# A graph-network kernel on one core: index tables and row statistics in one block, and convolutions whose carried edge sums go through TensorE

## The reference, cut to what matters

```
x = x + _L0_gnn_ref(_layernorm(x, axis=-1), src, dst, gamma, beta, W, b)
def _L0_gnn_ref(x, src, dst, gamma, beta, W, b):
    out_deg = clip(segment_sum(ones, src), 1.0); in_deg = clip(segment_sum(ones, dst), 1.0)
    for i in range(3):
        x = (x - mean(x, 0)) * rsqrt(var(x, 0) + EPS) * gamma[i] + beta[i]
        h = x * out_deg ** -0.5
        agg = segment_sum(h[src], dst) * in_deg ** -0.5
        x = relu(agg @ W[i] + b[i])
```

## Time and profile before

| what | value |
|---|---|
| median of 3 runs | 4209.92 us (4209.26 to 4211.09) |
| the profiled execution | 4210.74 us |
| its span, first to last instruction | 4209.0 us |
| mean granted TensorE clock | 0.89 of full speed |
| busy: PE, DVE, POOL, ACT | 3413.8, 2659.6, 1414.7, 1239.1 us |
| from the start to the end of the third round | 1144.1 us |

### The profile page before, as it was taken

How to read it: one execution, slowest core, us unless ns; L and a number is a source line. 1 busy time by engine, 2 the same in 40 slices (tenths; PEclk the granted TensorE clock), 3 DMA queues, 4 the chain that set the end, 5 groups by cost and what they waited for, 6 DMA issues and landing times. The chain is left out here.

```text
span 4209.0 us, 60863 instructions
## 1 busy us (share of the span) xinstructions
PE 3413.8 (81%) x16811; PEld 2667.0 (63%) x16812; DVE 2659.6 (63%) x6025; ACT 1239.1 (29%) x2287; POOL 1414.7 (34%) x1753
## 2 busy tenths in 40 slices
PE   4876377888877410899999999999949996688999
PEld 3610255666677410788888888888838884575766
DVE  7765797894367677454544545445428887776776
ACT  0122144452211100443443434344311111113443
POOL 0176387783255201132222222223113330006552
PEclk9999699999955555899999999999979998798999
DMA  1043222333399401454544534445322210126664
GB/s 51 0 126 80 63 93 83 110 97 120 118 310 310 150 0 36 131 143 102 144 124 113 134 102 137 128 107 142 95 71 60 58 55 17 74 94 147 160 156 107
DMA packets 254792, 457.41 MB, mean 109 GB/s; under 512 B 66065, under 2 KB 71482, under 8 KB 254064
## 3 DMA queue, kind: packets, MB, share of 16 engines
q1 hardware_dynamic: 180899, 288.95, 20.9%
q0 software_dynamic: 62368, 145.38, 15.8%
q10 hardware_dynamic: 11318, 20.54, 1.3%
HBM read 327.73 MB, written 126.85 MB: 108 GB/s over the span
## 5 line engine op out<-in xcount | busy, mean ns | idle before, releaser
L1336 PE MATMUL experts_psU<-experts_x_hi,experts_up_hi 128*128 128x312 f32 (+1 forms) x1408 | 436.8, 310 | 15.4 <-issue 11.8
L1337 PE MATMUL experts_psU<-experts_x_lo,experts_up_hi 128*128 128x312 f32 (+1 forms) x1408 | 436.6, 310 | 0.0
L1338 PE MATMUL experts_psU<-experts_x_hi,experts_up_lo 128*128 128x312 f32 (+1 forms) x1408 | 435.9, 310 | 0.0
L1350 PE MATMUL experts_psO<-experts_dn_hi,experts_hid_hi 128*104 128x512 f32 (+1 forms) x1056 | 421.5, 399 | 0.0
L1351 PE MATMUL experts_psO<-experts_dn_lo,experts_hid_hi 128*104 128x512 f32 (+1 forms) x1056 | 415.4, 393 | 0.0
L1352 PE MATMUL experts_psO<-experts_dn_hi,experts_hid_lo 128*104 128x512 f32 (+1 forms) x1056 | 415.4, 393 | 0.0
L1296 POOL DMA_INDIRECT experts_xg<-xn,experts_token_i x96 | 100.6, 1048 | 768.6 <-DVE experts_token_i L1432 749.1
L1464 DVE TENSOR_TENSOR experts_hid_lo<-experts_hid,experts_hid_hi 128x312 fp32r<-128x312 f32 (+1 forms) x352 | 161.6, 482 | 231.5 <-ACT experts_hid L1398 228.2
L1456 DVE TENSOR_TENSOR experts_dn_lo<-experts_dn_raw,experts_dn_hi 128x1536 fp32r<-128x1536 f32 (+1 forms) x128 | 207.9, 1624 | 122.5 <-ACT experts_dn_hi L1384 122.5
L1336 PEld LDWEIGHTS experts_psU<-experts_x_hi,experts_up_hi 128*128 128x128 f32 (+1 forms) x1408 | 265.4, 188 | 19.3 <-issue 17.3
L1396 ACT ACTIVATE experts_hid_hi<-experts_psU,experts_bup 128x312 fp32r<-128x312 f32 (+1 forms) x352 | 183.7, 522 | 296.7 <-PE experts_psU L1338 260.3
(11 more groups left out here) (391 smaller groups left out, 8506.9 us busy)
## 6 DMA issues: line engine op xcount, KB each, us to landing
experts_dn_raw<-in_L_ffn_W_down SPq DMA_DIRECT2D x96, 768.0 KB, 4.6
experts_up_raw<-in_L_ffn_W_up SPq DMA_DIRECT2D x32, 682.5 KB, 10.0
conv<-gcn_diff SPq DMA_DIRECT2D x80, 256.0 KB, 2.0
stats_xt<-in_x SPq DMA_DIRECT2D x78, 256.0 KB, 2.7
route_xt<-in_x SPq DMA_DIRECT2D x78, 256.0 KB, 4.8
x<-route_xt SPq DMA_DIRECT2D x78, 256.0 KB, 4.3
xn<-route_xn ACTq DMA_DIRECT2D x78, 256.0 KB, 4.8
two_xt<-x SPq DMA_DIRECT2D x78, 256.0 KB, 2.8
```

Source lines behind the costliest of these rows:

```text
L1336: pe.matmul(acc, up_hi[:, c, cols], x_hi[:, c, :], start=(c == 0), stop=False)
L1337: pe.matmul(acc, up_hi[:, c, cols], x_lo[:, c, :], start=False, stop=False)
L1338: mm = pe.matmul(acc, up_lo[:, c, cols], x_hi[:, c, :], start=False, stop=(c == C - 1))
L1350: pe.matmul(psO[0:S, q, :], hid_hi[0:w, m, s], dn_hi[0:w, m, :], start=(m == 0), stop=False)
```

## The change

`index_tables` and `records_and_stats` become one block, `index_and_stats`. Twelve node tiles get their statistics before the loop over the edge tiles begins, and two more in each turn (`AHEAD` = 12); their column sums follow four tiles behind (`LAG`), inside TensorE's turn. The normed rows are now made on ScalarE from a root and a shift that GpSimd computes. The lookups are turned around: the one-hot matrix is the lower part, transposed by TensorE (`turn`), and the tables are split into a high and a low bfloat16 part, so a lookup is four bfloat16 matmuls. The scatters follow in the same loop, four edge tiles behind, straight from the records.

In `gcn_tables` the scan and `link` for all partitions go; TensorE sums the columns of `adj`, and the weights of all three rounds are loaded here. In `gcn_layer` the carry moves into the closing matmul: the last tile's first row of `psZ` is copied into row 0 of `vb` by ScalarE (`carry`), its rest into row 32 by VectorE (`lower_carry`), and the next tile's closing matmul, now of 33 rows, adds them where the marks say so. `heighten` and `lower` read PSUM; relu and difference are one VectorE instruction; the running sums move from GpSimd to VectorE; the norm of the first round moves to ScalarE. GpSimd issues four gathers, not two, ahead of the power that opens the scale.

```diff
+def index_and_stats(nc, g, x, src, dst, attr, total, square):
+    R, S, G, AHEAD, LAG = 12, 6, 4, 12, 4
+        reached = lambda t, back: range(max(0, min(NT, AHEAD + 2 * t - back)), ...)
...
+        def _(act):
+                act.activation(xn[0:r, k, :], xt[0:r, j, :], ACT.Identity, bias=shift[0:r, j:j + 1],
+                               scale=rstd[0:r, j:j + 1]).then_inc(normed, 1)
...
+        def _(pool):
+            for t in range(ET):
+                for n in reached(t, 0):
+                    root(n)
+                if t >= G:
+                    if t % G == 0:
+                        grade(t // G - 1)
+                    scatter(t - G)
...
+        def _(pe):
+            for t in range(ET):
+                if t + 1 < ET:
+                    turn(t + 1)
+                    histogram(t + 1)
+                for stat in reached(t, LAG):
+                    add_up(stat)
+                pe.wait_ge(picked, t + 1)
+                pe.wait_ge(lowered, t + 1)
+                if t >= 2:
+                    pe.wait_ge(look_step, 5 * (t - 1))
+                for n, cols in enumerate((slice(0, 3), slice(3, 5))):
+                    for k in range(2):
+                        mm = pe.matmul(psL[:, j, cols.start * NH:cols.stop * NH], pick[:, j, n, :],
+                                       tabs[:, j, k, cols, :].rearrange("l c h -> l (c h)"), start=(k == 0), stop=(k == 1))
...
-            step(v.tensor_tensor_scan(wsum[:, ::-1], same[:, ::-1], wrow[:, ::-1], 0.0, ALU.mult, ALU.add))
-            pool.tensor_tensor(parts[:, 1, :], wsum[:, :], parts[:, 0, :], ALU.subtract).then_inc(split, 1)
+                pe.matmul(psW[0:1, k % 2, :], g.ones[:, 0:1],
+                          g.adj[:, k * G:(k + 1) * G, :].rearrange("p t l -> p (t l)"),
+                          start=True, stop=True).then_inc(summed, 1)
...
-            def add(s, j):
-                pool.tensor_tensor(total[:, :], total[:, :], headed[:, j, :], ALU.add)
-                pool.tensor_tensor(square[:, :], square[:, :], dsq[:, j, :], ALU.add).then_inc(added, 1)
-            for s in range(2):
+            for s in range(R):
                 gather(s, s)
             pool.wait_ge(moments, 1)
...
+            def close(s, j):
+                at_least(pe, wstaged, s, 0)
+                at_least(pe, carried, s, 1)
                 pe.matmul(psZ[:, j % 2, :], ws[:, j, :], vb[:, :], start=False, stop=True).then_inc(projected, 1)
-            tiles(pe, ET, [(0, aggregate), (3, project)], R)
+            tiles(pe, ET, [(L + 3, project), (L, aggregate), (L + 3, close)], R)
...
+            def carry(s, j):
+                act.copy(vb[0:1, :], psZ[0:1, j % 2, :]).then_inc(carry_high, 1)
+            tiles(act, ET, [(L + 4, carry)] + ([(1, norm)] if first else []) + [(L + 1, heighten), (L + 1, stage_w)]
+                  + ([] if last else [(L + 5, sq_diff)]), R)
...
-                    v.scalar_tensor_tensor(agg[:, j, h, :], g.link[:, tile(s), :], of, psA[:, j, h * P:(h + 1) * P],
-                                           ALU.mult, ALU.add).then_inc(carried, 1)
+                v.tensor_tensor(vb[32:33, :], psZ[0:1, j % 2, :], vb[0:1, :].bitcast(F32), ALU.subtract)\
+                    .then_inc(carried, 1)
+                    v.scalar_tensor_tensor(diff[:, j, :], psZ[:, j % 2, :], 0.0, bias, ALU.max, ALU.subtract)\
+                        .then_inc(differed, 1)
+            def add(s, j):
+                v.tensor_tensor(total[:, :], total[:, :], headed[:, j, :], ALU.add)
+                v.tensor_tensor(square[:, :], square[:, :], dsq[:, j, :], ALU.add).then_inc(added, 1)
+            tiles(v, ET, ([] if last else [(L + 6, add)]) + [(L + 4, lower_carry), (L + 4, differ), (L + 1, lower)]
+                  + ([(0, stats)] if first else []), R)
```

More of the change, by code:

```diff
@@ L323, in _ @@
[L323 to L338 removed]
+                v.sem_inc(hot, 1)
@@ L396, in gcn_tables @@
+        loaded, transposed, copied, stored, rows, step_done, one, linked, unlinked, weighed, summed, high, low, placed = (
+            ph.sem(n) for n in ("loaded", "transposed", "copied", "stored", "rows", "step", "one", "linked", "unlinked",
+                                "weighed", "summed", "high", "low", "placed"))
         block = ph.block()
```

771 lines of the change are left out of this document (406 added, 365 removed).

## The result

The changed kernel takes 4003.69 us (median of three runs, 4002.68 to 4007.54) against 4209.92: a ratio of 0.951, 95% interval 0.950 to 0.953, or 206 us less. I had forecast 4032, so the direction and most of the amount came as told, and the gain is 28 us larger than the sum said; the time lies a little nearer to rival (3), 3984 us, than to the forecast. The profiled execution is the slowest of the three: 4007.54 us, span 4005.8.

A forecast was written before the change was run, and what follows sets the result against it. GpSimd was taken to pace the old statistics, GpSimd sums holding VectorE to slow rounds one and two, TensorE to bound round three. Block 108, tables 8 and rounds 62 us less make 178: 4032 us, range 3975 to 4090.

The forecast's parts named there:

- rival (3): Everything overlaps better: block turns 5.0 us (27 us), round one at TensorE's 4.21 (15), tables 50 us (6): 3984 us; chance 0.13.
- New block: 108 said: Index tables and statistics as one block: ends at 298, taken as 300 us, against 408.2 before, 108 us less.
- loop start 62: New block: the loop over edge tiles reaches its first sum at 62 us, against 77.8 in the old lookup loop.
- turn 5.8: New block: each of 34 edge-tile turns with statistics takes 5.8 us, with bounds of 5.0 and 7.0.
- light turn 3.4: New block: each of the six turns without statistics takes some 3.4 us, 20 us together.
- the longest engine plus a little: New block's turn: VectorE 5.65 us, GpSimd 5.5 to 6.0, TensorE 4.7; the longest, slightly raised, gives 5.8 us.
- Round one: 39 said: Round one: VectorE's work sets closing matmuls 4.6 us apart (32.4 less); start 5 and end 1.6 less: 39.0 us.
- Rounds two and three: 21.5 and 1.5 said: TensorE's 4.21 us a tile decides; round two gains 21.5 us, round three 1.5 through its start and end.
- The carry at nothing: Rounds: the carry between closing matmuls takes 1.7 us within 3.7 us of TensorE work; 2 us cover remain, no cost.
- (1): New block: GpSimd paces it at 7.0 us a turn, 41 us less gain, 4073 us; chance 0.18.
- (2): Round one: GpSimd's root, shift and copy still stop VectorE through SBUF exclusion, up to 35 us, 4067 us; chance 0.12.
- (4): Rounds: the carry chain does not hide; above 3.7 us each us costs 120 us, at 5.5 us 4248 us; chance 0.05.

The follow-up runs named there:

- the four kernels: Changed kernel with statistics chains interleaved by two, GpSimd roots by two, both edits, or column sums two tiles behind: 4001.28, 3996.5, 3980.34 and 4092.55 us.
- mended: Changed kernel with statistics and roots by two, lower parts among tables-phase weights, earlier power in round one, ScalarE's norm behind the raised part: 3959.3 us, ratio 0.941.
- mended_f32: `mended` plus round one's statistics chain interleaved with the running sums, and float32 lookups in the new block: 3950.06 us, ratio 0.939.

## Why the prediction was right, and which terms were off

**New block: 108 said, 128 measured.** The mechanism held; the sizes, over the steps of the prediction: loop start 62, measured 57; turn 5.8, measured 5.18; light turn 3.4, measured 3.89; end of scatters and exit 19, measured 23.7 (256.5 to 280.2). That is -5, -21, +3 and +5 us on 298, and 2 more by which I rounded up. The first of these is a slip of counting: I had put the first sum at 62, where it came, 61.65, and then added all forty turns behind it, though the first of them was already in the 62. The turn is the term that counts. I added whole durations for VectorE, 5.65 us, and the trace shows instructions that begin 0.06 to 0.12 us before their forerunner ends; that is the lower bound of 5.0 that I had named and set aside. For GpSimd I said 5.5 to 6.0; it needs 4.77 us, and some 2.1 more in every fourth turn, 5.3 on average. My step "the longest engine plus a little" was wrong in kind: two engines were nearly equally long, as the four kernels show, and nothing was left over for a wait because sums run four tiles behind. The light turns are longer than said because GpSimd makes up there for what it is behind. Had the lag been two, the waits would have cost 2.5 us a turn.

**Tables: 8 said, 12.5 measured.** The sums in turn were foreseen at 1.4 us each and took 1.24; the larger part is the end: from the last lower part of a sum (327.36) to the next phase it took 4.7 us, where 8.8 were left for transfers and exit.

**Round one: 39 said, 36.5 measured, by another cause than I gave.** The first closing came 32.3 us after the start (32 said), the tail from the end of the last closing was 5.7 (9.7 said), closings 4.76 us apart (4.6 said). I derived 4.6 from VectorE's sum of work, 4.66 us, and took it for what decides. That step is the one that failed. The sum itself was right: in the middle of the round `mended` shows 4.62. But the ring set the distance, 4.92 there, and moving one entry of ScalarE's list took it away. Against that, the tiles at the start and the end of the round were faster than I allowed, which brings the mean to 4.76 with the ring and 4.43 without it. Two errors of opposite sign nearly cancel, so the number came out near by chance.

**Rounds two and three: 21.5 and 1.5 said, 25.3 and 4.0 measured.** Closings at 4.25 and 4.21 us are as said. The starts were 1.3 and 2.4 us shorter than said, the tail of round two 4.0 us shorter: with the sums on VectorE only two pairs are left behind the last closing.

**The carry at nothing:** right in rounds two and three, with 2.2 us to spare in round three, where it was tried. In round one TensorE waited 8.6 us for the low carry, 0.2 us a tile, because VectorE came late, not because the carry was long: with the same carry it waited 2.4 us in `mended` and nothing in `mended_f32`.

**The rivals.** (1) GpSimd at 7.0 us a turn: no, though it was one of the two bounds. (2) The exclusion in round one: it is there, but GpSimd is the one that stands still; its root took 1.08 us beside a running sum where it takes 0.57 alone, while no sum took over 0.70 us. It lengthened the ring by up to 0.5 us a tile and vanished from the total once the ring was cut (`mended` still has roots of 1.0 us). (3) All better: it came true in the turn, 21 of its 27 us, and in the tables, 4 of 6, but not in round one. (4) The carry: no.

## What to carry to other kernels

When taking work off the busiest engine gains nothing, do not conclude that it was not the bound: look for a second engine that is as full, and relieve both. When the distance between repetitions is near an engine's sum of work, follow one repetition step by step all the same; a ring through several queues, closed by an unrelated instruction that happens to stand ahead in one of them, can be cut by moving one entry of a list. An edit that pays nothing or costs something under one bound can pay under the next, so it is worth a second run after the bound has moved.

## What I had not expected of the hardware

GpSimd's power on one column was stretched to 3.75 us, and the shift behind it to 5.04, while VectorE built its one-hot tables from two SBUF operands (3.49 and 5.49 us); alone they take 0.57 and 0.27. It happened once, ahead of the loop, and no run shows what it cost the block:

```profile
30.76 3.49 DVE L434 TENSOR_TENSOR index_is_hi<-index_hi,all_count 128x3200 bf16<-128x3200 int32 x1
30.91 3.75 POOL L310 TENSOR_TENSOR index_rstd<-index_mv,all_minus_half 128x1 f32<-128x1 f32 x1 [0.23 <-DVE index_mv L135]
...
34.87 5.04 POOL L313 TENSOR_SCALAR index_shift<-index_mv,index_rstd 128x1 f32<-128x1 f32 x1 [0.21 <-POOL index_rstd L310]
```

A power over two columns took 0.75 us against 0.56 for one, and over eight 1.66: some 0.15 to 0.2 us a column on top of 0.4, so that putting columns together pays by the instruction saved and by its wait.
